# A decoder layer pair on one core: idle products on TensorE, norm sums by halves, another order in the last feed-forward

## What is computed

```python
x = _layernorm(x + _L0_attn_ref(...))    # windowed attention over 7 neighbours, 16 heads
x = _layernorm(x + _L0_xattn_ref(...))   # cross attention to the context
x = _layernorm(x + _L0_ffn_ref(...))     # 8 experts, each picks 16 of the 128 rows
x = _layernorm(x + _L1_attn_ref(...))    # attention with a decay mask
x = _layernorm(x + _L1_xattn_ref(...))   # each row takes its best context row as memory
x = _layernorm(x + _L1_ffn_ref(...))     # feed-forward, below
```

```python
h = bit_linear(x, w1)                     # rows quantized to 8 bits, weights to -1, 0, 1
h = depthwise_conv1d(h, conv_w, conv_b)   # three taps along the sequence
h = jax.nn.silu(h)
return bit_linear(h, w2)
```

## Time and profile before

| | |
|---|---|
| median of 3 runs | 1035.07 us (1033.67 to 1036.02) |
| the profiled execution's own time | 1034.66 us |
| its span, first to last instruction | 1032.9 us |
| PE busy | 915.1 us, 89% |
| DVE busy | 864.8 us, 84% |
| ACT busy | 744.9 us, 72% |
| POOL busy | 205.5 us, 20% |
| mean clock granted to PE | 0.970 |

### The profile page before, as it was taken

The page is one execution under the profiler, slowest core; times in us unless marked ns, Lnnn a source line. Parts: engine busy times, 40 slices in busy tenths (PEclk is TensorE's granted clock), DMA queues, the critical chain, the costliest instruction groups (busy, mean ns, idle before and its releaser), DMA issues.

```text
span 1032.9 us, 20266 instructions
## 1 busy us (share of the span) xinstructions
PE 915.1 (89%) x7382; PEld 666.8 (65%) x7382; DVE 864.8 (84%) x2216; ACT 744.9 (72%) x1857; POOL 205.5 (20%) x469
## 2 busy tenths in 40 slices
PE   6778998999999999999999999999999988897552
PEld 4566666767676776767775767768676756574331
DVE  4987668599898999899999999998999886868755
ACT  2375565777877878787878788777968787867643
POOL 2011221213131211313131312213131312110010
PEclk9989999999999999999999999999999999999765
DMA  8932221110303030211203030302102000000000
GB/s 269 370 80 82 71 61 32 46 47 22 92 1 113 1 112 1 71 42 52 62 11 102 1 92 22 110 3 68 46 31 72 22 1 21 2 22 2 11 10 11
DMA packets 36628, 59.06 MB, mean 57 GB/s; under 512 B 6656, under 2 KB 15872, under 8 KB 36016
## 3 DMA queue, kind: packets, MB, share of 16 engines
q1 hardware_dynamic: 36528, 57.76, 18.1%
HBM read 28.77 MB, written 4.19 MB: 32 GB/s over the span
## 4 chain that ended last, share of the span: by engine, by line
PE 54%; ACT 17%; DVE 16%; SPq 6%; issue 4%; POOL 3%; DMA 1%; ACTq 0%; POOLq 0%; DVEq 0%
PE bank_c L465 16%; PE banks_e L465 8%; PE bank_a L465 7%; PE bank_x L465 6%; DVE area_f L1319 4%; PE bank_f L465 3%; ACT area_e L1608 3%; DVE neg_top L1259 3%; ACT squares_out L1393 3%; SPq L435 2%; PE banks_e L843 2%; ACT area_f L1642 2%; PE bank_a L571 2%; PE bank_x L674 2%; DVE x L934 1%
## 5 line engine op out<-in xcount | busy, mean ns | idle before, releaser
L1319 DVE SCALAR_TENSOR_TENSOR area_f<-area_f,w_convw 128x254 f32<-128x254 f32 x256 | 111.7, 478 | 9.7 <-ACT area_f L1642 7.7
L1381 ACT ACTIVATE area_bx<-bank_x 128x512 f32<-128x512 f32 (+1 forms) x144 | 70.2, 499 | 22.3 <-PE bank_x L674 7.5
L1057 DVE TENSOR_TENSOR area_a<-area_a 128x512 f32<-128x512 f32 x112 | 73.0, 684 | 14.2 <-ACT area_a L1381 12.5
L1259 DVE TENSOR_REDUCE neg_top<-banks_e 128x8 f32<-128x1024 f32 x64 | 76.4, 1219 | 10.1 <-PE banks_e L465 9.9
L1642 ACT ACTIVATE area_f<-area_f,w_convb,w_convw 128x256 f32<-128x256 f32 x128 | 69.8, 595 | 17.8 <-DVE area_f L1310 17.6
L1608 ACT ACTIVATE area_e<-banks_e 128x512 f32<-128x512 f32 x128 | 69.1, 598 | 10.2 <-PE banks_e L843 10.1
L1112 DVE TENSOR_TENSOR area_a<-area_a 128x512 f32<-128x512 f32 x112 | 74.9, 684 | 1.7
L1116 DVE TENSOR_TENSOR area_a<-area_a 128x512 f32<-128x512 f32 x96 | 65.7, 684 | 0.3
L1381 ACT ACTIVATE area_a<-bank_a 128x512 f32<-128x512 f32 (+1 forms) x80 | 44.2, 552 | 26.2 <-PE bank_a L465 21.0
L1381 ACT ACTIVATE area_bx<-bank_c 128x512 f32<-128x512 f32 x64 | 34.7, 542 | 33.7 <-PE bank_c L465 26.3
L465 PE MATMUL bank_x<-area_bx 128*128 128x128 f32 (+1 forms) x256 | 51.6, 334 | 4.1 <-ACT area_bx L1381 3.1
(11 more groups left out here) (318 smaller groups left out, 2575.1 us busy)
## 6 DMA issues: line engine op xcount, KB each, us to landing
area_a<-area_a SPq DMA_DIRECT2D x96, 224.0 KB
area_a<-in_xT SPq DMA_DIRECT2D x16, 256.0 KB, 2.9
area_bx<-in_ctxT SPq DMA_DIRECT2D x16, 256.0 KB, 3.0
x<-in_x SPq DMA_DIRECT2D x16, 256.0 KB, 3.6
area_d<-in_ctxT SPq DMA_DIRECT2D x16, 256.0 KB, 2.7
y<-x SPq DMA_DIRECT2D x16, 256.0 KB, 2.2
w_wqkv_e<-in_wqkv_e SPq DMA_DIRECT2D x1, 3072.0 KB, 11.2
area_f<-in_raw SPq DMA_DIRECT2D x2, 1024.0 KB, 12.2
```

The source lines that it names most:

```text
L1057: return dve.tensor_tensor(product_of(wi).rearrange("p (n t) -> p n t", t=P), qT0.rearrange("p c (b t) -> p (c b) t", t=P), kT0.rearrange( ...
L1259: dve.tensor_reduce(top[:, b, r:r + 2, :, 0].rearrange("p r (par c) -> p r c par", c=DC), banks_e[:, r:r + 2, :].rearrange("p r (c par k) ...
L1319: last = dve.scalar_tensor_tensor(c4[:, i, :, dst], h4[:, i, :, src], cwt3[:, 2 * jj + i, k:k + 1], c4[:, i, :, dst], ALU.mult, ALU.add)
L1381: return act.activation(dst, src, ACT.Copy)
```

## The change

Five things:

1. **Products whose result nobody reads.** A new station W on PE, `warm`, makes `WARM` = 127 products of 128x512, bf16, into `bank_x`, which is free by then: it waits once until the experts of the last group are added. The letters W stand in PE's table, in ones to elevens, between the entries from the decayed station of the last group on to the last output product.
2. **Sums by halves.** `n.added` rises behind each of the two additions. ACT's square of the first half waits for the first one alone. All other waits on it count twice as far.
3. **The last feed-forward** (`LATE = 15`, so the last group alone): on ACT `middle` comes first and without a lag, then `magnitude`, then `tanh`; on DVE the order is `evacuated(at)`, `convolved(at - 1)`, `gated(at - 2)`, `largest(at - 3)`. An evacuation of the fourth block now waits for the gate of the first, in whose buffer it writes.
4. **The last norm**: ACT applies the scale to half 0 alone; DVE does half 1, and the store waits for both.
5. **The tables** of PE, DVE, ACT and POOL are different in many places by exchanges of entries. Leaving out the new letters, an entry of PE's table stands at most seven places from where it stood. SP's table is the same.

```diff
+WARM = 127
+LATE = 15
 ORDER = {
     "PE": (
-        "FECEXEDEXDFXDDFFDFDXFXECXCECFCXECFCEDXEXEDXEXFDXFEXDXDEDEFECECECFFFECEFCCFDFEEDEDEDFEDEFDEFEEFFFEEFEFEFE"
-        "EEFEFEFFFFFFFFFFFFF"
+        "FECEXEDEXFXDDDFFDFDXFXECXFCECFCXECCEDXEXEEXDXFDXFEXDXDEDEFECWEWWCEFCFWWFECWEFWWCWWWCWWFWEWFDWWWWWEWWDWWE"
+        "WDWWEDWWWFEWWDWWWEFDEWFEWWWWEWWFWWFFWWEEWFWWWWWWEWFWWEWWWFWEWWWWWWEWWWWWEWWWWFWEWFWEWWFWWWWWWWWWWWFWWWWW"
+        "FFWWWWFWWWWFWWWWWWWWFWWWWWWWWWWFWWFWWFFWFF"
...
 def feed_forward(g):                       # SP
     sp.wait_ge(n_f.done, g + 1)
+    if g == NG - 1:
+        sp.wait_ge(last_normed, 1)
...
-                until("a", n_a.added, g + 1)
+                until("a", n_a.added, GB * (g + 1))
...
+            def warm(_):
+                pe.wait_ge(n_x.added, GB * NG)
+                for i in range(WARM):
+                    pe.matmul(bank_x[:, :], ones_bf[:, :], bc(bias_parts[0][:, :], 1, GB), start=True, stop=True)
+                    yield
...
             def norm(n, x, bank, scale=None):
                 for b in range(GB):
-                    last = dve.scalar_tensor_tensor(x[:, b, :], bank[b], 1.0 if scale is None else scale[:, b:b + 1],
-                                                    x[:, b, :], ALU.mult, ALU.add, accum_out=n.sums[:, b:b + 1])
-                last.then_inc(n.added, 1)
+                    dve.scalar_tensor_tensor(x[:, b, :], bank[b], 1.0 if scale is None else scale[:, b:b + 1],
+                                             x[:, b, :], ALU.mult, ALU.add, accum_out=n.sums[:, b:b + 1]).then_inc(n.added, 1)
...
                 def evacuated(jj):
...
+                    if jj > 2:
+                        dve.wait_ge(f_silu, NJ * g + jj - 2)
...
+                if g == NG - 1:
+                    dve.wait_ge(n_f.scaled, n_f.steps * NG)
+                    dve.tensor_scalar(x[:, 1, :], x[:, 1, :], n_f.scale[:, 0, 1:2], n_f.scale[:, 1, 1:2],
+                                      ALU.mult, ALU.add).then_inc(last_normed, 1)
...
             def squares(n, x, g):
...
-                act.wait_ge(n.added, g + 1)
                 squares_by.append((n.squared, g + 1))
                 for b in range(GB):
+                    act.wait_ge(n.added, GB * g + b + 1)
...
-                for at in range(NJ + 3):
-                    for lag, step in ((3, magnitude), (2, tanh), (1, middle)):
+                lags = ((0, middle), (2, magnitude), (1, tanh)) if g >= LATE else ((3, magnitude), (2, tanh), (1, middle))
+                for at in range(NJ + 3):
+                    for lag, step in lags:
```

## The result

The changed kernel took 1024.12 us (median of 4 runs, 1022.71 to 1026.34), the kernel before on the same chip 1035.55 us (4 runs): a ratio of 0.989, with a 95% interval of 0.9865 to 0.9915, or 11 us less. The forecast was 1026.8 us, with a range of 1020.5 to 1032.5. The profiled execution took 1023.55 us with a span of 1021.8 us, 11.1 us under the span before.

What follows compares the result with a forecast made beforehand. The body was taken as bound by PE, the end by chains through PE, ACT and DVE with PE's clock at 0.50. -3.6 - 1.7 - 0.6 - 0.5 - 1.5 = -7.9 from 1034.66 gives 1026.8 us; range 1020.5 to 1032.5.

Steps and rivals of the forecast that it cites:

- The clock in the stage: Memory of group 15 beside feed-forward of group 14 (957 to 997 us): added products hold PE's clock at 1.00; -3.6 us.
- The two smaller terms: Same stage: squares no longer wait for the sum's second half (0.4 us saved); added products ahead of due work cost 0.5.
- DVE is late next: Last memory step: its norm queues on DVE behind feed-forward 14's gating products, so starts 3.7 us earlier instead of 5.
- The reordering: Last feed-forward, first evacuation to last maximum: new order leaves DVE 1.9 us of waiting instead of 3.7; stage -1.7 us.
- To the evacuation: Start of the last feed-forward, at full clock: fp16 transposes give 0.2 us and the first product 0.4; -0.6 us.
- The end: Output product and last norm: idle product +0.4, earlier squares -0.4, norm half on DVE -0.5; in all -0.5 us.
- The body: 0 to 957 us: moved table entries and earlier squares give -1.5 us, bounds -7 to +6.
- The third rival: Body gains what it could: 0.5 us a group, -6.5 us, 1021.8 us in all; chance 0.17.
- the second rival: Body slower: PE entry that waits set ahead of ready ones, 0.7 us more a group, 1037.4 us; chance 0.06.
- The first rival: Last stages: clock doesn't hold and added products cost instead, 1035.9 us; chance 0.09. One fall, 1029.3 us, counted to the forecast.
- PE's busy time: Whole kernel: sign to look for, PE's busy time up by some 27 us.

Runs made afterwards that it cites:

- last order only: The kernel before with only the last feed-forward's new order (scale first on ACT, evacuation first on DVE); 1034.88 us, ratio 0.9995.
- experiment 5: The kernel before with the 127 idle products alone, at the same places of PE's table; 1031.89 us, ratio 0.9968.
- experiment 1: The changed kernel without its 127 idle products, all else as it is; 1028.22 us, ratio 0.9934 to the kernel before.
- experiment 6: Same run as last order only: the kernel before with the last feed-forward's new order alone, in the tables of before; 1034.88 us, ratio 0.9995.
- experiment 3: The kernel before with the sums and squares handed on by halves alone, in its own order; 1034.65 us, ratio 0.9983.
- experiment 4: The kernel before with halves and new tables together, no idle products, last feed-forward as before; 1029.65 us, ratio 0.994.
- 8: The changed kernel with 45 instead of 10 idle products behind the last feed-forward's last product; 1023.48 us, ratio 0.9886 to the kernel before.
- experiment 7: The changed kernel with every second idle product left out, 64 instead of 127; 1024.85 us, ratio 0.9905 to the kernel before.

## Why the prediction was right, step by step

**The clock in the stage: right.** Each piece came out as priced (the earlier trace rows against the rows after). Up to the norm it was 4.1 us instead of 3.7. The two smaller terms can be read singly: from norm to maximum of x it is 4.84 us before, 5.19 with the idle products alone and 4.79 with the halves too, so the products cost 0.35 us there (0.5 priced) and the halves give 0.4 (0.4 priced). The stage was -4.1, forecast -3.6. What was taken for one number, however, isn't one: without the products this stage took 37.95 to 39.57 us in six kernels (39.57, 39.51, 38.17, 38.15, 38.12, 37.95), depending on where the clock fell. The two ends, before and last order only, have the same order on every engine up to there: in the first the values of the first half ran at full clock (1.07 us) and those of the second at half (1.93), in the other it was the reverse (1.94 and 1.06). Against before the products give 3.74 us (experiment 5), against experiment 1 only 2.7, and against last order only 2.1. The forecast was made against an execution at the long end of this, so that the size came out so near is in part luck.

**DVE is late next: right.** The gating products end at 983.91 us and the norm starts at 983.83 with no idle time.

**The reordering: right in size and in reason.** 15.4 us were forecast (its own working adds up to 15.3, 13.4 of work and 1.9 of waits) and 15.42 measured; the walked waits of 0.86 us (the second evacuation) and 0.7 (the last gate) read 0.70 and 0.61. Of the 1.68 us, 1.27 are the order (experiment 6) and 0.43 the clock (15.85 against 15.42). To the evacuation it was -0.59, forecast -0.6.

**The end: -0.8 instead of -0.5.** From addition to end it was -0.88 for a forecast of -0.9: 0.4 by the halves (7.14 to 6.73 in experiment 3) and some 0.5 by the split of the norm (6.70 to 6.20, experiment 4 against 1). The idle product inside the output product takes 0.43 us of PE, as forecast (products at 1013.32 and 1014.18 us). But the clock rose behind it (0.50 up to 1014.5 us, 0.74 in the next half), and the last two pairs came 0.30 and 0.22 us behind the ones before instead of 0.42. On balance +0.06. The kernels without this product show 7.08 to 7.33 us at the low clock, those with it 7.16 and twice 7.34, so no gain of it is shown there.

**The body: right in sign, too small.** This is the term that was mis-sized: -1.5 forecast, -4.5 measured in the body and -3.9 up to the first scores of group 15, inside the bounds of -7 to +6. It makes up 2.4 of the 3.2 us by which the sum missed the profiled execution. The third rival, with -6.5 us in the body and 1021.8 us in all, is nearer to the 1023.55 us of the profiled execution than the forecast of 1026.8. The prediction looked at the halves and the tables one by one, and singly they bring -1.9 and 0. It said that ACT seldom waits for the sums in the body; the list above has 23 such waits, 24.0 us in all. It said that PE has under 3 us of waits a group to lose; that is true, and 0.35 us a group (4.5 by 13) did go. What was missed is that an order may be good only with another edit: the tables set PE's transposes behind a norm that the halves make earlier. This accounts for 2.3 of the 5.0 us between the tables alone and both (experiment 4); why the body gains the rest stays open. The mechanism of the second rival (an entry that waits is set ahead of ready ones) did happen: PE's wait for the normed x went from 2.1 to 7.3 us with the tables alone. It was made up for elsewhere in PE's queue, and in sum came out at zero, not at +0.7 us a group.

**The first rival** did not come true in the profiled execution, and in part in others: one fall in experiments 5 and 8 and, with half of the products, short ones in experiment 7. The Trainium skill (TensorE: Matmul & The Clock Gate, section "A second HAM failure mode: psum-queue depth-cycling") spoke for it; here the clock held over groups of 1 to 11 products with waits of up to 2.23 us between them.

**PE's busy time: wrong.** It rose by 16.1 us, not by 27. The 127 products are 27.9 us by themselves at 0.22 us; the forecast left out that PE's own instructions get shorter at the full clock (projection 3.40 to 1.99 us, and so on), although its sum for the stage rests on just that.

## What to carry to other kernels

Where a chain of short matmuls waits for other engines at the end of a kernel, unused products in the waits can keep the clock up; price them by what stands behind them in PE's queue, and look for the engine that is late next, here DVE with its queue. A new order and an edit that makes data come earlier must be priced and tried together: here 0 and -1.9 us gave -4.9. An edit of about 1 us is read from its own stretch of the trace and not from times that spread by 3 us or more, but only where that stretch repeats: from first evacuation to last maximum it did to 0.02 us, in the stage ahead of it only to 1.6 us.

## What the runs showed of the hardware that was not expected

**The same order can run at either clock.** The values of the second half stand behind the same wait of 2.23 us, with the same idle products ahead of them, in the kernel after (at 975.45 us, 1.06 us long, shown above) and in the kernel with the clock held to the end:

```profile
976.83 1.89 PE L471 MATMUL banks_e<-area_e,chosen_v 128*32 128x512 f32 x8 [2.23 <-ACT area_e L1640]
978.65 2.08 PE L933 MATMUL bank_x<-bias_parts,ones_bf 128*128 128x512 bf16 x5
```

PE's order up to there is the same in both. In the second one the clock read 0.97 in the microsecond up to 977 us and 0.50 in the three behind it. The stage took 0.8 us more for it. What decides between the two was not found.

**The start differs from profile to profile.** The first norm of the experts lies between 103.0 and 106.8 us, while the parts behind it repeat closely in kernels with the same edits (body 848.9 to 849.5 us in six of them). PE's clock from 50 to 60 us read 0.80 in before, 0.84 in after, 0.50 without idle products, 0.51 with the tables alone and 1.00 with the last order alone. The start does not follow it: 0.50 goes with 103.4 us (no idle products) and 1.00 with 106.7 (last order alone). What makes this spread stays open. With one profile of each kernel, how much of the 2 to 6 us by which the times of one kernel differ comes from the start was not measured.
